# A graph network on one core: GpSimd's gathers with two gates a block in place of thirteen and ten

## The reference

```
def layer0(feat, efeat, W_e, b_e, bias, src, dst):
    ew = (efeat @ W_e + b_e).reshape(E, 16, 16)
    msg = einsum('ei,eio->eo', feat[src], ew)
    summed, cnt = segment_sum(msg, dst), segment_sum(ones(E), dst)
    return summed / maximum(cnt, 1.0)[:, None] + bias
def layer1(features, src, dst, edge_type, edge_emb, w_ih, w_hh, b_ih, b_hh):
    msg = einsum('emh,eh->em', edge_emb[edge_type].reshape(-1, 16, 16), features[src])
    m = segment_sum(msg, dst)
    return gru(m, features)                   # gates r, z, n
x = layernorm(x + layer0(x, edge_attr_16, ..., src, dst))
x = layernorm(x + layer1(x, src, dst, edge_type_8, ...))
```

## Time and profile before

| | |
|---|---|
| time, three runs | 5720.92 us median, 5718.9 to 5726.7 |
| profiled execution | 5721.4 us, its span 5719.6 us |
| granted TensorE clock, mean of the span | 0.989 |
| TensorE busy (matmuls / weight loads) | 90% / 81% |
| VectorE, ScalarE, GpSimd busy | 73%, 68%, 59% |
| stage 0, blocks | about 42 to 2,830 us of the span |
| stage 1, blocks | about 2,900 to 5,650 us |

### The profile page before, as it was taken

One profiled execution on the slowest core, in us unless ns is written; L12 is line 12 of the kernel. 1 busy time (PEld: TensorE's weight loads), 2 busy tenths in 40 slices (PEclk: granted clock), 3 DMA queues, 4 the chain that ended last, 5 costly groups with the idle time before them and its releaser, 6 DMA issues.

```text
span 5719.6 us, 131035 instructions
## 1 busy us (share of the span) xinstructions
PE 5142.5 (90%) x41758; PEld 4642.5 (81%) x41759; DVE 4200.5 (73%) x5387; ACT 3887.2 (68%) x5533; POOL 3397.9 (59%) x3559
## 2 busy tenths in 40 slices
PE   6999999999999999999878888888888888888887
PEld 5888888888888888888768888787888878788886
DVE  7888888888888888888856666666666666666666
ACT  6667677767777667766566666666666666667664
POOL 6555556556556556555556666666666656666664
PEclk9999999999999999999989999999999999999998
DMA  3111111111111111111111111111111111111110
GB/s 67 30 33 32 33 31 32 32 32 33 31 31 33 32 33 31 33 31 32 27 20 24 24 24 24 24 22 24 24 24 24 24 24 23 25 22 24 24 23 14
DMA packets 330970, 161.25 MB, mean 28 GB/s; under 512 B 193244, under 2 KB 330011, under 8 KB 330771
## 3 DMA queue, kind: packets, MB, share of 16 engines
q1 hardware_dynamic: 218224, 130.59, 9.2%
q0 software_dynamic: 112512, 29.03, 5.7%
q10 hardware_dynamic: 160, 0.80, 0.1%
HBM read 157.44 MB, written 2.66 MB: 28 GB/s over the span
## 4 chain that ended last, share of the span: by engine, by line
PE 77%; issue 12%; DVE 8%; DVEq 2%; another core or an unknown queue 1%; ACT 0%; POOL 0%; DMA 0%; ACTq 0%; SPq 0%
PE psN L752 59%; PE psM L789 15%; DVE cand L953 3%; DVE z L991 2%; PE psM L770 1%; PE psM L760 1%; DVE z L959 1%; DVEq L997 1%; DVE nodeT L935 1%; PE psM L771 0%; DVEq L934 0%; PE psM L773 0%; PE psM L761 0%; PE psN L893 0%
## 5 line engine op out<-in xcount | busy, mean ns | idle before, releaser
L752 PE MATMUL psN<-table_hi,pick 128*128 128x320 f32 (+1 forms) x13670 | 4047.3, 314 | 159.9 <-issue 107.5
L752 PE MATMUL psN<-table_lo,pick 128*128 128x320 f32 (+1 forms) x13670 | 3965.8, 306 | 9.4 <-issue 9.0
L752 PEld LDWEIGHTS psN<-table_hi,pick 128*128 128x128 f32 x13670 | 2579.1, 189 | 282.4 <-issue 222.5
L578 ACT ACTIVATE pick<-dist 128x640 fp32r<-128x640 bf16 (+1 forms) x2485 | 1788.0, 782 | 1263.0 <-PE psN L752 670.2
L752 PEld LDWEIGHTS psN<-table_lo,pick 128*128 128x128 f32 x13670 | 2580.9, 189 | 11.9 <-issue 10.8
L500 POOL DMA_INDIRECT z<-in_x,idx x1761 | 1685.8, 957 | 1131.4 <-PE psN L752 441.6
L500 POOL DMA_INDIRECT z<-h_rows,idx x1755 | 1685.7, 961 | 1116.4 <-issue 421.3
L570 ACT ACTIVATE dist<-src_mod,neg_node 128x640 bf16<-128x640 uint16 (+1 forms) x2485 | 1968.6, 868 | 4.6 <-DMA src_mod<-src_mod_rows 4.6
L953 DVE TENSOR_TENSOR cand<-psN,grp_hot 128x640 f32<-128x640 f32 (+1 forms) x1492 | 1123.7, 765 | 960.6 <-PE psN L752 630.4
L991 DVE TENSOR_TENSOR z<-psD,z 128x2048 f32<-128x2048 f32 (+1 forms) x750 | 1367.6, 1823 | 55.3 <-issue 31.4
L789 PE MATMUL psM<-z,onehot 128*32 128x273 f32 (+1 forms) x12500 | 845.3, 339 | 321.0 <-issue 266.7
(11 more groups left out here) (108 smaller groups left out, 771.5 us busy)
## 6 DMA issues: line engine op xcount, KB each, us to landing
src_mod<-src_mod_rows SPq DMA_DIRECT2D x249, 192.0 KB
src_mod<-src_mod_rows SPq DMA_DIRECT2D x248, 160.0 KB
z<-in_x,idx POOLq DMA_INDIRECT x1761
z<-h_rows,idx POOLq DMA_INDIRECT x1755
eab<-in_edge_attr SPq DMA_DIRECT2D x125, 200.0 KB
idx<-in_src SPq DMA_DIRECT2D x250, 12.5 KB
dstb<-in_dst SPq DMA_DIRECT2D x250, 14.0 KB
grp<-src_grp SPq DMA_DIRECT2D x249, 5.5 KB
```

Source lines behind the costliest of these rows:

```text
L578: act.activation(pick[j][:, CHUNKS[i], 0:hi - lo], dist[i][:, 0:hi - lo], ACT.Relu, bias=1.0, scale=-1.0).then_inc(l["pick_act"], 1)
L752: mm = pe.matmul(rows[:, :, 0:cells.shape[2]], pick[j][:, c, at:at + P], cells, start=(i == 0 and part == 0), stop=(i == TC - 1 and part = ...
```

## The change

Only the three tables change. In both stages `AFTER_OWN` becomes empty; `AFTER_LAST` keeps one gate, before n=0, on pick 8 of the block before; `AFTER_SUMS` stays at column 7 in stage 1 and goes from column 10 to 8 in stage 0. So each block has two gates: the gathers n=0 to 7 (stage 1: 0 to 6) follow each other behind the first, and n=8 to 13 (7 to 13) behind the second.

```
-AFTER_OWN = ([{4: 0, 5: 1, 6: 2, 7: 3, 8: 4, 11: 5, 12: 6}] * 2, [{5: 0, 6: 1, 9: 3, 10: 4, 12: 5}] * 2)
-AFTER_SUMS = (10, 7)
-AFTER_LAST = ([{0: 7, 1: 8, 2: 9, 3: 10}] * 2, [{0: 7, 1: 8, 2: 9, 4: 10}] * 2)
+AFTER_OWN = ([{}] * 2, [{}] * 2)
+AFTER_SUMS = (8, 7)
+AFTER_LAST = ([{0: 8}] * 2, [{0: 8}] * 2)
```

## The result

The changed kernel takes 6292.22 us (median of four runs, 6282.47 to 6298.54) against 5723.81 of the kernel before: a ratio of 1.0994, 95% interval 1.0981 to 1.1007. Its profiled span is 6285.1 us, 565.5 longer. The forecast was slower, by 190 us; it is three times that.

What follows compares the result with a forecast made beforehand. TensorE, busy 90%, left little room; the block loops hung on its signals, late behind gather runs. 5721 + 44 (stage 1) + 149 (stage 0) = 5914, stated as 5910 us; range 5640 to 6270.

Steps and rivals of the forecast that it cites:

- Mechanism: Both stages: while gathers go back to back, TensorE's signals come late, mostly some 1.2 us after the run's end.
- Stage 0, up to add_run: Stage 0, start of a block's sums to VectorE's add_run: 14.04 us after the change, 1.66 later than before.
- S: The time at which the sums of a stage 0 block start; later events in the block are counted from it.
- Stage 0, from add_run to the next sums: Stage 0, VectorE's cands and TensorE's picks: 9.81 us as before, less 0.29 free; stage 0 in all +149 us.
- Rival C: Both stages: signals held to the run's end and sums stopped as behind the run of 12; 6562 us, chance 0.08.
- 0.6 us of stutter: Stage 0 sums: added because the first run of eight gathers reaches about 2.0 us into them; sums through at S+5.3.
- Stage 1 has a precedent in its last blocks: Stage 1: last blocks already ran seven and seven gathers, cand passing in mid-run; period 22.60 us, +44 us in all.
- 24.61: Stage 1, upper bound of the period in us (22.09 + 2.52) if nothing passes in mid-run; +291 us.
- rival B: Both stages: faster, as gathers no longer start inside the sums; 5627 us, up to 5700 if less comes; chance 0.23.
- Late data at nothing: Stage 0, column 8 gathered some 2.5 us later against its sums: counted 0, bounds 0 and 0.3 us a block.
- SP's queue at nothing: SP's loads of later indices shift with the gathers by some two microseconds, but no gather waits for them: 0.
- Gates at nothing: The removed gate instructions on GpSimd, which isn't the bound and idles 41%: counted 0.

## Why the prediction was wrong: two terms of the right mechanism were too small

- **Mechanism: right.** Long runs hold TensorE's signals back until some 1.6 us behind their end; shown by the dates of the signals, by the pauses, which bring most of the time back without another gate, and by the kernel with fewer gathers.
- **Stage 0, up to add_run: right.** Gate at S+5.6 and add_run at S+14.04 were forecast; the block above has 5.37 and 14.18, the mean add_run is S+13.80.
- **Stage 0, from add_run to the next sums: the step that failed.** That "the next sums come 9.8 after it" was carried over from the block of before, and 9.52 stood in the sum, with 0.29 called free. The mean is 11.71 (10.2 before). The run of eight holds not only signals but TensorE itself, ahead of the sums: it stands 2.64 us a block among its picks (1.91 on issue, the rest for a cand or for ScalarE's one-hot rows), 0.04 before. Rival C came nearest to this, but held the sums up and not the picks ahead of them; the forecast had charged the first run with 0.6 us of stutter in the sums. (25.47 - 23.56) x 123 = 235 us.
- **Stage 1: the other step that failed** is "Stage 1 has a precedent in its last blocks". The cand passed in mid-run there; in the 117 blocks ahead it came at the run's end, and gate to add_run took 12.1 us (4487.46 to 4499.60) instead of the precedent's 10.22. The prediction named what was different ("less other traffic") and was wrong in that as well: it is not the loads. The bound it had worked out beside, 24.61, was as near (0.96 too high, against 1.05 too low); what kept the stage below it is that the sums got cleaner, 2.12 us from first to last matmul against 3.62, which was rival B's point. (23.65 - 22.60) x 123 = 129 us.
- With these two, 5910 + 235 + 129 = 6274, against 6292 measured; that is an account and no test, as both periods are measured. The rule of the Trainium skill by which TensorE never waits ("SBUF — State Buffer", section "Who interferes with whom") would have given no change; the kernel with fewer gathers, where TensorE's gaps vanish, speaks against it in this use.
- **Late data at nothing: right**, by the waits of the outer products, 31.4 us before and after. **SP's queue at nothing: right** for the kernel before (1.0009 with two of the loads cut), and at most 1.7 points in the changed one. **Gates at nothing** was not tested by itself.

## What to carry to other kernels

A wait that guards no data can still be worth its place: before removing one, ask what the stretch without work behind it lets through. Where gathers run beside a tight loop of other engines, look for signals that come together just behind the end of a run, and cut the runs where such a signal is on the path; a gate does that only if it is shut when it is reached. And a precedent taken from the first or last blocks of a loop is from other code than the loop's: check in the bulk of the blocks whether the same thing occurs there, before it sizes a term.

## What the runs showed of the hardware

- While GpSimd issued gathers (128 rows each, 0.96 us and 0.30 between two) back to back, TensorE's signals to VectorE in a loop came 1.6 us behind the last one's end, in 117 of 119 blocks at the same 10.0 to 10.5 us after the start of a run of seven. VectorE's and ScalarE's own signals were not held (0.01 us). TensorE stood too, and resumed with the release (1.14 and 1.00 us in the blocks above).
- Gaps of 1.31 us between runs of three and four gathers gave nearly all of the loss back (1.0077 against 1.0994); 0.80 us did so in part (1.0571).
- Written-out code on TensorE, VectorE and ScalarE took half of the effect away in the changed kernel (1.0994 to 1.0472), on TensorE alone a fifth (1.0778), and it changed nothing in the kernel before (0.9991).
- A smaller part of the loss in stage 1 may be TensorE's clock. Its mean grant over the span fell from 0.989 to 0.961. Behind a stand of 1.75 us that ends at 4596.95, the clock granted from 4597.97 to 4601.50 is 0.54, near the lower of its two levels (1.2 and 2.4 GHz), and matmuls of the picks start 0.27 us apart instead of 0.147. There are some seven such matmuls a block, one or two before: 0.6 us a block, if all of them lay on the path, which no run shows.
